# Unpaced slot scatters, a later last batch and single row loads in an attention and mixture-of-experts kernel

## The chip, the cores and the metric

The kernel runs on one core of one Trainium2 chip. The metric is the device time of one execution in microseconds. Three runs of the kernel before gave 550.91, 548.15 and 549.37 us, a median of 549.37.

## What is computed

The input x has 8 batches of 1024 tokens with 128 features, in float32. Two layers follow each other, each with a residual sum:

```
x = x + layernorm(linear_attention(layernorm(x)))          # 16 heads of 8
u = layernorm(x)
logits = (layernorm(u)*ln_scale + ln_bias) @ gate_w.T      # 8 experts
w      = the two largest softmax values, renormalised; 0 for the other experts
y = swiglu(u; shared weights) + sum_e w[:, e] * swiglu(u; Wg[e], Wu[e], Wd[e])   # 128 -> 256 -> 128
x = x + layernorm(y)
```

Each token goes to only two of the eight experts, so 16,384 token rows are computed instead of 65,536.

## The kernel before, in words

**Attention and routing.** Batches go through steps 0 to 7. In a step TensorE (PE) computes attention for one batch, and for the batch before it the shared expert and the router's logits. VectorE (DVE) finds each token's two experts, and a product with a triangular matrix (`ranks`) gives each token its place among the rows of its expert. GpSimd (POOL) then runs `scatter(k)` (line 555) for batch k: 16 indirect DMAs of 128 rows of 144 floats each, which put every token row into `slots_dram`, once for each of its two experts, at the rows named in `slot_i`. They rotate over four semaphores (`lane_out`, LANES = 4). `slots_ready` tells POOL that a batch's slots are known.

**Expert units.** The rows are worked off in 72 units of 256 rows. Units 0 to 31 (N1 = 32) take rows of batches 0 to 4 (FIRST = 5), units 32 to 71 the rest. For a unit n, PE transposes x three units ahead (line 795), multiplies by the gate and up weights (line 806), and multiplies unit n-2 by the down weights (line 816). ScalarE (ACT) copies the transposed x (line 981), takes the silu (line 898), and scales the output into one of four buffers `yb` of four units (line 995). DVE multiplies silu and up (line 1151, `hidden`). POOL writes the output with two indirect DMAs of 128 rows each (`scatter_y`, line 580) to `routed_dram`, where the two results of a token lie side by side.

**Order around the change.** Each engine works its instructions in order, and the order is written out by hand. POOL's is: slot scatters of batches 0 to 5, outputs of units 0 to 3, slot scatters of batch 6 (SEVENTH), outputs of units 4 to 15, slot scatters of batch 7, outputs of units 16 to 71. Within units 0 to 31 the routing of the last two batches is woven in: RANKS_OF names the units ahead of which PE computes `ranks` for batches 6 and 7; T_AT, LOGITS_AT and COUNT_AT those of batch 7's two transposes (line 702), its logits (line 709) and the final count of rows per expert (line 767). On DVE the pieces start at MAIN_FROM, ROUTER_FROM, WEIGHTS_FROM, SLOTS_FROM and TABLE_FROM and advance by up to six steps a unit. On ACT, U_AFTER, UT_AFTER and EXP_AFTER place the corresponding work. Between units 31 and 32 stand the shared expert's products of batches 6 and 7 (`late_stages`, lines 670 and 691).

**The load queue.** SyncE (SP) issues all plain DMAs. After the up product of unit n it loads the weights of unit n+4 (256 KB, `load_weights`, line 421, four places) and the rows of unit n+8 (`load_unit`, line 426). At n = PADS_AFTER it waits for `pads_ready` and issues eight writes of pad rows (`load_pads`, line 433). Rows for units 32 to 39 are loaded after the pads and all slot scatters have landed. At n = 55 it waits until the outputs of 48 units have landed and then issues the row loads of the final stage (`load_pair`, line 439, 1024 KB each, four places). The load of batch 4 is to wait for `pair_read` 1, since it reuses the place of batch 0. Loads of batches 5 to 7 follow once every output scatter has landed.

**The final stage.** From unit 58 on (C_FROM) DVE advances it by up to three steps after each unit (C_STRAND): `c_sums` adds the two results of a token (line 1583), adds the shared expert's output (line 1587) and takes statistics (line 1591). `c_norm` scales (line 1005 on ACT, 1619 on DVE), `c_add` adds the residual (line 1627), and SP stores.

Of the kernel before, what the change touches and what calls it, by code (L numbers as in the profile page):

```python
# [20 lines left out]
B, S = 8, 1024  # L21
NT = S // P
# [14 lines left out]
SLOTS_C = 4  # L37
LANES = 4
# [9 lines left out]
FIRST = 5  # L48
# [19 lines left out]
STRAND = 6  # L68
SPLIT_STEP = 47
SEVENTH = B - 2  # L70
RANKS_OF = {5: SEVENTH, 19: B - 1}
T_AT = (13, 14)
LOGITS_AT = 15
COUNT_AT = 21
X_AHEAD = 3
SLOTS7_FROM = 5
MAIN_FROM = 5
ROUTER_FROM = 15
WEIGHTS_FROM = 18
SLOTS_FROM = 19  # L80
TABLE_FROM = 21
U_AFTER = 12
UT_AFTER = (13, 14)
EXP_AFTER = {4: SEVENTH, 17: B - 1}
SCATTER_AFTER = (4, 16)
PADS_AFTER = 25
TABLE1_AT = tuple(range(1, 36, 2))
C_LOAD_AT = (55, 60)
C_FROM = 58
C_STRAND = 3  # L90
C_NORM_AFTER = (66, 67)
# [8 lines left out]
def program(nc, x, w_qkv, b_qkv, w_proj, b_proj, ln_scale, ln_bias, gate_w, wg, wu, wd, swg, swu, swd, out):  # L100
# [13 lines left out]
    with ctx:  # L114
# [6 lines left out]
        def sem(name):  # L121
            return ctx.enter_context(nc.semaphore(name))
# [185 lines left out]
        lane_out = [sem("lane_out0"), sem("lane_out1"), sem("lane_out2"), sem("lane_out3")]  # L308
# [20 lines left out]
        def pair(b):  # L329

            places = [wgu[1][:, i * NE // 2:(i + 1) * NE // 2, :].rearrange("p e n -> p (e n)") for i in range(2)]
            places += [pad_rows[:, :, :].rearrange("p e n -> p (e n)")[:, 0:2 * NT * E], u_rows_[:, :, :, :].rearrange("p a t n -> p (a t n)")[:, 0:2 * NT * E]]
            return places[b % SLOTS_C].rearrange("p (t c n) -> p t c n", c=2, n=E)
# [42 lines left out]
        def _(sp):  # L376
# [42 lines left out]
            def load_weights(n):  # L419
                e = sp.value_load(unit_ei[0:1, n:n + 1], min_val=0, max_val=NE - 1)  # L420
                sp.dma_start(w_unit(n), wgu_dram[ds(e, 1), :, :].rearrange("e p n -> p (e n)")).then_inc(w_in[n % WSLOTS], 16)

            def load_unit(n):
                i = n % QU
                row = sp.value_load(unit_row[0:1, n:n + 1], min_val=0, max_val=SLOTS - W)
                sp.dma_start(xb[i // HALF][:, TILES * (i % HALF):TILES * (i % HALF) + TILES, :],
                             slots_dram[ds(row, W), :].rearrange("(p t) n -> p t n", t=TILES)).then_inc(xb_in[i], 16)

            def load_pads():
                sp.wait_ge(pads_ready, 1)  # L430
                for e in range(NE):
                    row = sp.value_load(pad_i[0:1, e:e + 1], min_val=0, max_val=NE * CAP - W)
                    sp.dma_start(slots_dram[ds(row, W), :].rearrange("(p t) n -> p (t n)", t=TILES),
                                 pad_rows[:, TILES * e:TILES * e + TILES, :].rearrange("p t n -> p (t n)")).then_inc(pads_in, 16)

            def load_pair(b):
                if b >= SLOTS_C:
                    sp.wait_ge(pair_read, b - SLOTS_C + 1)
                sp.dma_start(pair(b).rearrange("p t c n -> p (t c n)"), routed_v[b, :, :]).then_inc(pair_in[b % SLOTS_C], 16)
# [18 lines left out]
            for n in range(UNITS - WSLOTS):  # L458
                sp.wait_ge(up_ps, n + 1)
                if n + WSLOTS == N1:  # L460
                    sp.wait_ge(table_ready, 2)
                load_weights(n + WSLOTS)
                if n == PADS_AFTER:
                    load_pads()
                if n % HALF == 0:
                    sp.wait_ge(yi_sb, n // HALF + 1)
                if n + QU < N1 or N1 <= n < UNITS - QU:
                    load_unit(n + QU)
                if n == N1 - 1:
                    sp.wait_ge(pads_in, 16 * NE)  # L470
                    for lane in lane_out:
                        sp.wait_ge(lane, 16 * (2 * NT // LANES) * B)
                    for i in range(QU):
                        load_unit(N1 + i)
                if n == C_LOAD_AT[0]:

                    for place in y_out:
                        for done in place:
                            sp.wait_ge(done, 16 * HALF * (FIRST_DONE // HALF // YB))
                    for b in range(SLOTS_C):  # L480
                        load_pair(b)
                if n == C_LOAD_AT[1]:
                    load_pair(SLOTS_C)

            for place in range(YB):
                for done in y_out[place]:
# [9 lines left out]
        def _(pool):  # L496
            g = nc.gpsimd
            n = [0]
# [56 lines left out]
            def scatter(k, par):  # L555
                pool.wait_ge(slots_ready, k + 1)
                for i in range(2 * NT):
                    t, c = divmod(i, 2)
                    at = k * 2 * NT + i
                    if k < SEVENTH and i % LANES == 0 and at:  # L560
                        for lane in lane_out:
                            pool.wait_ge(lane, 16 * (at // LANES))
                    if k == SEVENTH and i == 0:
                        for lane in lane_out:
                            pool.wait_ge(lane, 16 * (at // LANES))
                    elif k >= SEVENTH and i % 2 == 0:

                        for one in (at - 3, at - 2):
                            pool.wait_ge(lane_out[one % LANES], 16 * (one // LANES + 1))
                    g.indirect_dma_start(slots_dram, bass.IndirectOffsetOnAxis(ap=slot_i[par][:, c * NT + t:c * NT + t + 1], axis=0),  # L570
                                         u_row[par][:, t, :], None).then_inc(lane_out[i % LANES], 16)

# [22 lines left out]
        def _(pe):  # L595
# [159 lines left out]
            def last_batch(n):  # L755

                m = B - 1
                if n in T_AT:
                    transpose_u(m, m % 2, [T_AT.index(n)])
                if n == LOGITS_AT:  # L760
                    pe.wait_ge(uT_sb, 2 * B)
                    logits(m)
                if n in RANKS_OF:
                    ranks(RANKS_OF[n])
                if n == COUNT_AT:
                    pe.wait_ge(oh_ready, B + 1)
# [111 lines left out]
        def _(act):  # L878
# [81 lines left out]
            def last_batch(n):  # L960

                m = B - 1
                if n == U_AFTER:
                    u_of(m, m % 2)
                if n in UT_AFTER:
                    uT_of(m, UT_AFTER.index(n))
                if n in EXP_AFTER:
                    router_exp(EXP_AFTER[n])

# [71 lines left out]
        def _(dv):  # L1041
# [460 lines left out]
            def second_last(m):  # L1502

                yield from slots(m, m % 2)
                yield from weights(m, m % 2)
# [128 lines left out]
            def last_stage():  # L1634
# [24 lines left out]
                for g in range(C_HELD + 1, len(C_GROUPS)):  # L1659
# [7 lines left out]
                    if g == last_g:  # L1667
# [6 lines left out]
            tail = weights(m, m % 2)  # L1674
            pieces = [(0, seventh, min(RANKS_OF)), (SLOTS7_FROM, second_last(SEVENTH), T_AT[0]), (MAIN_FROM, main(B, B % 2), T_AT[0]),
                      (ROUTER_FROM, router(m, m % 2), max(RANKS_OF)), (WEIGHTS_FROM, some(tail, 5), N1),
                      (SLOTS_FROM, closing(m, tail), COUNT_AT), (TABLE_FROM, table2(), PADS_AFTER)]
            dv.wait_ge(sy_ps, 2 * (B - LATE))
# [46 lines left out]
```

## Time and profile before

| | |
|---|---|
| Time of the profiled execution | 550.29 us |
| Its span, first to last instruction | 548.6 us |
| Median of three runs | 549.37 us |
| PE busy | 428.6 us (78% of the span) |
| DVE busy | 344.0 us (63%) |
| POOL busy | 277.1 us (51%) |
| ACT busy | 273.3 us (50%) |
| Mean granted clock of PE | 0.939 |

The shares are averages over very different stretches: PE has no work from about 501 us on, and POOL has little but slot scatters until 268 us. A timeline row gives the start, the duration, and in brackets the idle time ahead of it and what ended that. POOL's durations are those of preparing an indirect DMA; the transfer lands later.

### The profile page before, as it was taken

The numbers are of one execution on the slowest core, as the hardware profiler recorded it, in microseconds if no ns is written. First come the engines' busy times: TensorE is split into PE (matmuls) and PEld (weight loads), VectorE is DVE, ScalarE is ACT, GpSimd is POOL, SyncE is SP. The second block draws the span as 40 slices with busy tenths as digits, with TensorE's granted clock in tenths as the row PEclk, the third lists the DMA queues.
The fourth block names the chain that finished last, engine by engine and source line by source line (L and its number), as shares of the span: only waits on it lengthen the run. The fifth ranks groups of instructions, "written<-read, shape, count | busy, mean of one in ns | idle before, by whom it ended". The sixth has DMA issues, their size and how long they took to land.

```text
span 548.6 us, 9418 instructions
## 1 busy us (share of the span) xinstructions
PE 428.6 (78%) x2503; PEld 343.0 (63%) x2511; DVE 344.0 (63%) x1495; ACT 273.3 (50%) x627; POOL 277.1 (51%) x330
## 2 busy tenths in 40 slices
PE   0875979888798979788997999799999995995000
PEld 0453646566556646467996999656999994995000
DVE  6587888889798887984572484122323224886197
ACT  2452465654637474644754655333555552476504
POOL 6000003555453555535655677567777777778300
PEclk9987999999999999997999999999999998999555
DMA  8970000111010111135765565514767679841472
GB/s 254 313 253 0 1 2 23 44 45 43 33 45 34 43 45 38 39 109 164 201 183 150 158 191 195 163 60 133 220 183 204 197 212 410 261 138 45 167 278 115
DMA packets 41623, 73.93 MB, mean 135 GB/s; under 512 B 8803, under 2 KB 23782, under 8 KB 40422
## 3 DMA queue, kind: packets, MB, share of 16 engines
q1 hardware_dynamic: 32870, 54.48, 33.0%
q0 software_dynamic: 8704, 18.89, 9.5%
q8 instruction: 19, 0.31, 0.3%
q14 instruction: 30, 0.25, 0.1%
HBM read 45.82 MB, written 27.53 MB: 134 GB/s over the span
## 4 chain that ended last, share of the span: by engine, by line
PE 51%; DVE 17%; DMA 8%; ACT 8%; issue 6%; POOL 5%; SPq 4%; DVEq 1%; POOLq 0%
PE bank_g L806 9%; PE bank_p L806 8%; PE bank_h L816 8%; POOL routed_dram L580 5%; PE bank_p L653 4%; PE bank_g L670 3%; PE bank_h L691 3%; PE bank_p L614 3%; DVE hid_s L1162 3%; PE bank_t L795 2%; PE bank_h L670 2%; PE bank_t L709 2%; DMA wgu_slots<-wgu_dram 2%; PE bank_t L658 2%; DMA keep<-in_L_attn_x 2%
## 5 line engine op out<-in xcount | busy, mean ns | idle before, releaser
L570 POOL DMA_INDIRECT slots_dram<-u_rows,slot_i x128 | 123.4, 964 | 191.1 <-issue 105.8
L806 PE MATMUL bank_g<-xbT,wgu_slots 128*128 128x256 f32 x288 | 76.2, 388 | 8.0 <-DMA wgu_slots<-wgu_dram 6.2
L816 PEld LDWEIGHTS bank_h<-wdn,hid_s 128*128 128x128 f32 x576 | 75.3, 192 | 4.4 <-issue 0.8
L816 PE MATMUL bank_h<-wdn,hid_s 128*128 x576 | 75.8, 275 | 0.4 <-issue 0.4
L806 PE MATMUL bank_p<-xbT,wgu_slots 128*128 128x256 f32 x288 | 75.6, 386 | 0.0
L806 PEld LDWEIGHTS bank_p<-xbT,wgu_slots 128*128 128x128 f32 x288 | 55.9, 194 | 7.9
L1151 DVE TENSOR_TENSOR hid_s<-act_s,bank_p 128x512 f32<-128x512 f32 x36 | 24.7, 687 | 54.7 <-PE bank_p L806 49.1
L1151 DVE TENSOR_TENSOR hid_s<-q_e,bank_p 128x512 f32<-128x512 f32 x36 | 24.7, 685 | 53.5 <-PE bank_p L806 49.2
L806 PEld LDWEIGHTS bank_g<-xbT,wgu_slots 128*128 128x128 f32 x288 | 50.3, 195 | 12.4 <-DMA wgu_slots<-wgu_dram 6.4
L580 POOL DMA_INDIRECT routed_dram<-pk,yi x40 | 40.8, 1020 | 12.2 <-issue 10.7
L580 POOL DMA_INDIRECT routed_dram<-pqT,yi x40 | 39.8, 996 | 12.2 <-issue 11.6
L653 PE MATMUL bank_p<-wqkv,xnT 128*128 128x256 f32 x128 | 38.2, 399 | 0.0
L580 POOL DMA_INDIRECT routed_dram<-wgu_slots,yi x32 | 31.9, 997 | 9.8 <-issue 6.7
L580 POOL DMA_INDIRECT routed_dram<-att,yi x32 | 31.7, 992 | 9.8 <-issue 7.9
L1078 DVE BATCH_NORM_STATS2 st_r<-keep 128x6 f32<-128x128 f32 x128 | 30.4, 282 | 4.2 <-DMA keep<-in_L_attn_x 3.4
L1005 ACT ACTIVATE keep<-keep,shift,r_c 128x128 f32<-128x128 f32 x56 | 21.9, 483 | 22.1 <-DVE shift L1608 22.1
L981 ACT ACTIVATE xbT<-bank_t 128x256 f32<-128x256 f32 x72 | 27.4, 384 | 10.7 <-PE bank_t L795 10.7
L911 ACT ACTIVATE xn<-keep,nb_r,r_r 128x128 f32<-128x128 f32 x64 | 25.4, 481 | 10.9 <-DVE nb_r L1225 10.9
L652 PE MATMUL bank_p<-bias_bf,ones_bf 128*128 128x256 bf16 x64 | 18.3, 287 | 15.1 <-DVE pqT L1132 13.7
L670 PE MATMUL bank_g<-uT,swgu 128*128 128x512 f32 x56 | 29.3, 604 | 0.8 <-issue 0.8
L898 ACT ACTIVATE act_s<-bank_g 128x512 f32<-128x512 f32 x36 | 21.5, 597 | 14.8 <-PE bank_g L806 14.8
L670 PE MATMUL bank_h<-uT,swgu 128*128 128x512 f32 x56 | 27.9, 601 | 0.0
(258 smaller groups left out, 879.6 us busy)
## 6 DMA issues: line engine op xcount, KB each, us to landing
wgu_slots<-wgu_dram SPq DMA_DIRECT2D x72, 256.0 KB, 2.9
xn<-slots_dram SPq DMA_DIRECT2D x36, 144.0 KB, 2.8
v<-slots_dram SPq DMA_DIRECT2D x36, 144.0 KB
keep<-in_L_attn_x SPq DMA_DIRECT2D x8, 512.0 KB, 4.3
pair_rows<-routed_dram SPq DMA_DIRECT2D x4, 1024.0 KB, 6.1
out_dram<-keep SPq DMA_DIRECT2D x8, 512.0 KB, 7.6
wgu_dram<-keep SPq DMA_DIRECT2D x2, 1024.0 KB, 5.3
slots_dram<-u_rows,slot_i POOLq DMA_INDIRECT x128, 2.3
```

The source lines that it names most:

```text
L570: g.indirect_dma_start(slots_dram, bass.IndirectOffsetOnAxis(ap=slot_i[par][:, c * NT + t:c * NT + t + 1], axis=0), u_row[par][:, t, :], N ...
L580: g.indirect_dma_start(routed_dram, bass.IndirectOffsetOnAxis(ap=yi[:, h % (2 * YB), at:at + 1], axis=0), yb[h % YB][:, at, :], None).then ...
L653: last = mm(o, xnT[:, t * P:(t + 1) * P], wqkv[:, E:3 * E], start=False, stop=True)
L670: last = mm(bank[:, :], swgu[:, which * INTER + c * P:which * INTER + (c + 1) * P], uT_at(m)[:, half * 512:(half + 1) * 512], start=True, ...
L806: last = mm(bank[i % 2][:, c * W:(c + 1) * W], w_unit(i)[:, which * INTER + c * P:which * INTER + (c + 1) * P], xbT[:, i % XDEEP, :], star ...
L816: last = mm(bank[:, t * E:(t + 1) * E], hid[:, i % XDEEP, c * W + t * P:c * W + (t + 1) * P], wdn[:, ds(e, 1), c * E:(c + 1) * E].rearrang ...
L898: A(act_g[n % XDEEP], bank_g[n % 2][:, :], ACT.Silu).then_inc(silu, 1)
L911: ins = A(xn[:, t, 0:E], kept(f, t * E, (t + 1) * E), ACT.Identity, bias=nb_r[par][:, NT + t:NT + t + 1], scale=r_r[par][:, 2 * NT + t:2 * ...
L981: A(xbT[:, n % XDEEP, :], x_bank(n)[:, 0:W], ACT.Copy).then_inc(xbT_sb, 1)
L1005: ins = A(y, y, ACT.Identity, bias=shift[:, g % 2, at], scale=r_c[:, g % 2, at])
L1078: k = inc(v.bn_stats(st(t), src(t)))
L1151: v.tensor_tensor(hid[:, n % XDEEP, :], act_g[n % XDEEP], bank_p[n % 2][:, :], ALU.mult).then_inc(hid_sb, 1)
```

## The change

The waits inside the slot scatters of batches 5, 6 and 7 are left out: only the wait ahead of the first one of a batch is kept. In the kernel before, batch 5 waited ahead of every fourth, and batches 6 and 7 ahead of every second. The pieces of the last batch's routing are placed in later units: the transposes at units 14 and 16, logits at 18, ranks at 21, the count at 24, pads after 27, with their counterparts on DVE and ACT. Row loads of batches 0 to 4 in the final stage are issued one each at n = 55, 57, 59, 61 and 63, where four stood at 55 and one at 60.

```diff
-RANKS_OF = {5: SEVENTH, 19: B - 1}
-T_AT = (13, 14)
-LOGITS_AT = 15
-COUNT_AT = 21
+RANKS_OF = {5: SEVENTH, 21: B - 1}
+T_AT = (14, 16)
+LOGITS_AT = 18
+COUNT_AT = 24
-ROUTER_FROM = 15
-WEIGHTS_FROM = 18
-SLOTS_FROM = 19
-TABLE_FROM = 21
+ROUTER_FROM = 18
+WEIGHTS_FROM = 21
+SLOTS_FROM = 22
+TABLE_FROM = 24
-UT_AFTER = (13, 14)
-EXP_AFTER = {4: SEVENTH, 17: B - 1}
+UT_AFTER = (14, 16)
+EXP_AFTER = {4: SEVENTH, 20: B - 1}
-PADS_AFTER = 25
+PADS_AFTER = 27
-C_LOAD_AT = (55, 60)
+C_LOAD_AT = (55, 57, 59, 61, 63)
...
-                    for b in range(SLOTS_C):
-                        load_pair(b)
-                if n == C_LOAD_AT[1]:
-                    load_pair(SLOTS_C)
+                if n in C_LOAD_AT:
+                    load_pair(C_LOAD_AT.index(n))
...
-                    if k < SEVENTH and i % LANES == 0 and at:
+                    if i % (LANES if k < FIRST else 2 * NT) == 0 and at:
                         for lane in lane_out:
                             pool.wait_ge(lane, 16 * (at // LANES))
-                    if k == SEVENTH and i == 0:
-                        for lane in lane_out:
-                            pool.wait_ge(lane, 16 * (at // LANES))
-                    elif k >= SEVENTH and i % 2 == 0:
-
-                        for one in (at - 3, at - 2):
-                            pool.wait_ge(lane_out[one % LANES], 16 * (one // LANES + 1))
```

## Rows read from the trace of the kernel before

**Rows 1.** Page: rate of data in 40 slices; chain that ended last, by engine.
```profile
GB/s 254 313 253 0 1 2 23 44 45 43 33 45 34 43 45 38 39 109 164 201 183 150 158 191 195 163 60 133 220 183 204 197 212 410 261 138 45 167 278 115
...
PE 51%; DVE 17%; DMA 8%; ACT 8%; issue 6%; POOL 5%; SPq 4%; DVEq 1%; POOLq 0%
```

**Rows 2.** PE timeline, gate products of units 11, 12, 18 and batch 7's pieces.
```profile
283.73 1.03 PE L806 MATMUL bank_g<-xbT,wgu_slots 128*128 128x256 f32 x4
...
286.57 1.03 PE L806 MATMUL bank_g<-xbT,wgu_slots 128*128 128x256 f32 x4
...
290.59 0.65 PE L702 MATMUL bank_t<-ident,u_rows 128*128 128x128 f32 x4 [1.23 <-DVE u_rows L1237]
...
300.05 1.95 PE L709 MATMUL bank_t<-gate_c,xnT 128*128 128x8 f32 x16 [1.20 <-ACT xnT L920]
...
310.62 1.03 PE L806 MATMUL bank_g<-xbT,wgu_slots 128*128 128x256 f32 x4
```

**Rows 3.** DVE timeline: slots of batch 6 ready, experts of batch 7, slots ready.
```profile
274.14 0.17 DVE L1331 SCALAR_TENSOR_TENSOR u_rows<-r_exp,wden 128x8 f32<-128x8 f32 x1
...
310.90 0.23 DVE L1303 TENSOR_TENSOR oh_bf<-oh 128x64 bf16<-128x64 f32 x1
...
318.53 0.17 DVE L1331 SCALAR_TENSOR_TENSOR u_rows<-r_exp,wden 128x8 f32<-128x8 f32 x1
```

**Rows 4.** PE timeline: gate product of unit 30.
```profile
346.62 1.10 PE L806 MATMUL bank_g<-xbT,wgu_slots 128*128 128x256 f32 x4 [1.88 <-issue]
```

**Rows 5.** SP timeline: the eight pad writes, weights of units 57 and 60.
```profile
334.62 8.47 SPq L433 DMA_DIRECT2D slots_dram<-pad_rows  x8
...
440.60 0.33 SPq L421 DMA_DIRECT2D wgu_slots<-wgu_dram  x1
...
452.39 0.35 SPq L421 DMA_DIRECT2D wgu_slots<-wgu_dram  x1
```

**Rows 6.** PE timeline: gate products of units 60 and 61.
```profile
464.15 2.08 PE L806 MATMUL bank_g<-xbT,wgu_slots 128*128 128x256 f32 x4 [6.16 <-DMA wgu_slots<-wgu_dram]
...
468.81 1.03 PE L806 MATMUL bank_g<-xbT,wgu_slots 128*128 128x256 f32 x4
```

**Rows 7.** Page, DMA issues: KB each, median us to landing.
```profile
wgu_slots<-wgu_dram SPq DMA_DIRECT2D x72, 256.0 KB, 2.9
...
pair_rows<-routed_dram SPq DMA_DIRECT2D x4, 1024.0 KB, 6.1
```

**Rows 8.** POOL groups by line, 238 to 268.5 us: slot scatters of batch 5.
```profile
L570 POOL DMA_INDIRECT slots_dram<-u_rows,slot_i x16 | 15.3, 957 | 19.1 <-DMA slots_dram<-u_rows,slot_i 10.4 <-DVE u_rows L1331 5.1 <-issue 3.7
```

**Rows 9.** POOL timeline: first scatters of each stretch, a slow one, the last.
```profile
279.13 0.95 POOL L570 DMA_INDIRECT slots_dram<-u_rows,slot_i  x1 [0.30 <-issue]
...
308.80 0.96 POOL L580 DMA_INDIRECT routed_dram<-pqT,yi  x1 [0.30 <-issue]
...
339.71 0.96 POOL L570 DMA_INDIRECT slots_dram<-u_rows,slot_i  x1 [0.30 <-issue]
...
366.60 0.95 POOL L580 DMA_INDIRECT routed_dram<-pk,yi  x1 [0.30 <-issue]
...
407.01 0.96 POOL L580 DMA_INDIRECT routed_dram<-pk,yi  x1 [0.30 <-issue]
...
494.33 2.02 POOL L580 DMA_INDIRECT routed_dram<-pk,yi  x1 [0.30 <-issue]
...
512.11 0.95 POOL L580 DMA_INDIRECT routed_dram<-pqT,yi  x1 [0.30 <-issue]
```

**Rows 10.** ACT timeline: output of unit 68, normalisation after unit 71.
```profile
496.74 0.63 ACT L995 ACTIVATE pqT<-bank_h,yw 128x128 f32<-128x128 f32 x2 [1.16 <-PE bank_h L816]
...
502.13 12.40 ACT L1005 ACTIVATE keep<-keep,shift,r_c 128x128 f32<-128x128 f32 x32
```

**Rows 11.** DVE timeline: a residual sum, first sum after the last loads.
```profile
494.31 1.21 DVE L1627 TENSOR_TENSOR keep<-keep 128x1024 f32<-128x1024 f32 x1
...
519.76 1.23 DVE L1583 TENSOR_TENSOR pair_rows<-pair_rows 128x1024 f32<-128x1024 f32 x1 [10.05 <-DMA pair_rows<-routed_dram]
```

## The prediction, written before the changed kernel ran

> **What bounds the kernel now.** I read the page's shares and the chain of waits first, then the timelines of PE, POOL and SP around the three edits, then the end. The chain's shares say mostly PE [rows 1], but the reader is to see that two engines take turns. PE sets the pace up to its last down product near 501 us. The end is POOL's: the output scatter of unit 71 starts only at 512.11 [rows 9], though ACT wrote its output before 502.13, where its next work begins [rows 10]. POOL is some 10 us behind. Loads of batches 5 to 7 wait for that last scatter, DVE waits for them until 519.76 [rows 11], and a fixed tail of 548.6 - 519.76 = 28.8 us follows. So what counts is when POOL's last scatter ends, and that is the later of two things: POOL's own backlog, and PE's production of the last outputs. The change touches both.
>
> POOL's backlog comes from the slot scatters. Back to back, POOL needs (407.01 - 366.60) / 32 = 1.263 us a scatter [rows 9], 2.53 us for a unit's two. PE needs 286.57 - 283.73 = 2.84 us a unit [rows 2], so POOL gains only 0.31 us a unit and never makes up what it lost.
>
> **The scatters without pauses.** Sixteen at 1.263 are 20.2 us. Batch 5 has 10.4 us of waits for its own earlier scatters [rows 8]; the usual gap of 0.3 stays at three places, so 9.5 go. It then would reach unit 0's output before ACT has written it: here PE and ACT are the cover, and outputs 0 to 3 are set by them. Batch 6 next needs its slots, ready at 274.14 + 0.17 = 274.3 [rows 3]. So batch 6 starts at 274.5 instead of 279.13 and ends at 294.7 instead of 308.80 [rows 9]. Outputs 4 to 15 keep their 339.71 - 308.80 = 30.9 us, which gives 325.6. Are batch 7's slots ready by then? They were ready at 318.7, in unit 19, which starts one unit of 2.84 after 310.62 plus about 0.3 for the ranks, 313.7; that is 5.0 after its start [rows 2, 3]. Moved to unit 22 (three units later, 8.5 us) and with the 3.0 us that PE wins below, they are ready at 324.2, 1.4 us before POOL asks. Batch 7 runs from 325.6 to 345.8 instead of 366.60: POOL is 20.8 us ahead. Outputs 16 to 31 end at 386.2 instead of 407.01.
>
> How a run of 16 slot scatters without a wait behaves, no row shows: batch 5 has only four in a row. From below, they could run at the 1.263 of the output scatters, 64 KB each against 72. From above, nothing is gained and a batch takes the 29.7 (batch 6) or 26.9 us (batch 7) of now [rows 9]. I take 1.263: the output scatters go 32 in a row at it beside the same weight loads. Moving 72 KB per 1.26 us is 58 GB/s more, where the slices of this stretch show 130 to 220 and one slice reaches 410 [rows 1].
>
> A rule speaks against this. The Trainium skill (DMA: Bandwidth & Descriptors, "Issuing engines are not separate DMA queues") says that DMAs from all issuers end up on the same 16 DMA engines and interleave. By it alone denser scatters could delay the weight loads. That case is the last rival; the sum above stands without it.
>
> **The last batch's routing, two units apart.** Units 12 to 18 take 310.62 - 286.57 = 24.05 us. Six units are 17.04, and the pieces themselves 0.65 twice and 1.95, 3.25 together; 3.8 is left, of which three waits (1.23 for DVE's rows, one alike, 1.20 for ACT's copy) are nearly all [rows 2]. With the transposes at 14 and 16 and logits at 18, PE comes 2.84 us after DVE's and one or two units after ACT's part, so all 3.8 go. Late next are the ranks: before, they stood two units after the router's last unit, now one (router in 18 to 20, ranks at 21). In unit 17 (start 307.8, one unit before 310.62) DVE finished the expert masks at 311.1, 3.3 us after the start [rows 2, 3]; PE would ask after 2.6 (a unit without the two transposes), so it waits 0.7. Both bounds: 0 if DVE is a bit quicker, 2.0 if its pieces lag by a further product. I take 0.8 with the restart. Behind PE's wait only its own transposes queue. Net 3.0.
>
> The pads: on SP the eight writes take 8.47 us [rows 5] and stood ahead of the weights of unit 30; PE then idles 1.88 [rows 4]. Now they come after the weights of unit 31, the last that PE needs before the late shared products, which give more than 20 us of cover for units 32 to 35. The stall goes, 1.9. SP's waits for all slot scatters, formerly until batch 7 landed, now end near 348 and no longer come last; the eight unit loads behind them keep their place ahead of unit 32. DVE's table finishes in unit 26, before n = 28 needs it. The idle goes to 0 in the good case and stays 1.9 in the bad one. PE is then 4.9 us earlier at unit 32.
>
> **The row loads.** Before, four loads of 1 MB stood in SP's queue ahead of the weights of unit 60, issued at 452.39 [rows 5] and landed 11.7 later, where 2.9 is usual [rows 7]. PE idled 6.16, then ran unit 60 at the lower clock: 468.81 - 464.15 = 4.66 instead of 2.84, 1.8 more [rows 6]. Together 8.0. With one load ahead of the next weights the landing must stay below 8.8 us: unit 60 was due at 464.15 - 6.16 = 458.0, so unit 53 started seven units of 2.84 before, at 438.1; its turn's weights were issued at 440.60 [rows 5], 2.5 after, and are needed four units, 11.36, after the start. Four cost 11.7 - 2.9 = 8.8, so one costs 2.2, and 5.1 us is covered. In two units SP and POOL move 1.05 + 0.52 + 0.29 + 0.26 = 2.1 MB in 5.68 us, 375 GB/s, close to the 410 seen [rows 1], so this is the least sure term: between 8.0 and 0, and at the bad end four stalls. I take 8.0. DVE uses batch b three units after the unit whose turn issues it. The issue comes some 4 us after that unit's start (its weights at 2.5, then a unit load, about 1.5 for both: an estimate), DVE's use at 8.5 + 2.5; that leaves 7 us for a landing of 6.1 [rows 7]. Where a load lands at 8, DVE waits about a microsecond, and PE has a unit's slack before it needs the next `hidden`. So zero, up to 2 if the slack is used up. The 48-unit wait ahead of the loads no longer stops SP, since POOL has caught up by then.
>
> **The sum.** PE is 4.9 + 8.0 = 12.9 us earlier at the end. POOL reaches output 32 at 386.2. Output 68 was ready near 497.1 [rows 10]; 36 units of 2.84 and the 8.0 before it, output 32 was at 386.9, and 4.9 less is 382.0. It is 4 us behind, and closes that in 4 / 0.31 = 13 units. From then on POOL follows PE. Output 68 is ready at 496.74 + 0.37 - 12.9 = 484.2 [rows 10]; from it eight scatters come faster than PE's pace allows POOL to rest, 8 x 1.263 = 10.1, so the last ends at 494.0. Some scatters beside DVE's wide sums take longer: the one at 494.33 took 2.02 us instead of 0.96, and the sum at 494.31 ran exactly beside it [rows 9, 11]. For these I add 1.8, bounds 0 and 4. The last scatter ends at 495.8 instead of 513.06, 17.3 us earlier. ACT's 12.4 us of normalising after unit 71 end at 502.13 - 12.9 + 12.4 = 501.6, before DVE's first late sum at 502.5, so the tail moves along whole.
>
> A page disagrees with the 1.8. The Trainium skill (SBUF — State Buffer, "Who interferes with whom") holds that a `tensor_tensor` with both inputs in SBUF takes the read interface only, and infers that making descriptors does not need it, so such a sum would not stall an indirect DMA. By that rule the sum is 1.8 us lower. This trace's 2.02 speaks against it, and I go by the row.
>
> Profiled execution: 550.29 - 17.3 = 533.0. That execution is 0.92 above the median of the runs, so 532.1 is my number for the median.
>
> **The rivals.**
> 1. The forecast, 532.1: chance 0.66. Its own range is 529.5 (no slow scatters, no ranks wait) to 537 (4 us of slow scatters, 2.7 lost in ranks or a short stall).
> 2. One weight load still comes late. Rate near 375 GB/s speaks for it, the 5.1 below 8.8 against it. PE then wins only 4.9 at the end, and perhaps pays a stall of the clock: output 68 at 492.2, last scatter 503.8, 9.3 earlier, 540. Chance 0.17.
> 3. The unwaited scatters run no faster, because POOL itself is held when too many are under way. POOL stays 20 us behind: its last scatter remains at 513 minus 0 to 4, and 546 to 549 follows. The 32 output scatters in a row speak against. Chance 0.06. That a wait remains elsewhere (the change doing nothing) belongs here.
> 4. A better split: batch 7's slots earlier and all waits smaller, 528.5. Chance 0.06.
> 5. Slower. DVE stands in order, and each row load arrives after DVE's turn. If each lands 11 us after issue, as the weights behind four did, DVE waits 4.2, PE loses about that plus 1.8 for the clock, five times: 30 us, less the 17.3, 562. It decides against the change once DVE's waits pass 17 us in sum, 3.5 a load. By the interleaving rule above denser traffic makes this likelier. Chance 0.05.
>
> **How the numbers follow.** The range takes in the forecast, case 4 and most of case 2: 528.5 to 541, leaving out about 0.16. A measurement of this kernel can tell about 0.5%, 2.7 us, from no change. Faster: 0.66 + 0.17 + 0.06 and a third of case 3 give 0.91; same 0.04; slower 0.05.
>
> **What would show it.** Right: L570's 16 scatters of batches 5 to 7 at 1.26 spacing with no DMA releaser; L702 and L709 without idle; unit 30 without idle; no idle on PE at unit 60 and PEclk at full there; POOL waiting for ACT outputs from about unit 45 on; last scatter at 496. Wrong: idle before a gate product released by `wgu_slots`, DVE idle before line 1583 during units 60 to 68, or POOL still without waits to the end.

## The result, and the profile after

Three runs of the changed kernel took 533.62, 534.76 and 533.83 us, a median of 533.83 where 532.1 was predicted. Against the kernel before (549.37) that is a ratio of 0.9714 [0.9692, 0.9736]: faster, and inside the range. The profiled execution took 533.62 us with a span of 531.9, against 550.29 and 548.6, so 16.7 us are to be found. Line numbers are 9 lower than before from the scatters on, because the waits are gone: L561 is the slot scatter, L571 the output scatter, L797 the gate product.

From the page: the rate of data in 40 slices and the chain by engine. Against [rows 1] POOL's share of the chain fell from 5% to 2% and that of DMA from 8% to 5%, and PE's rose from 51% to 60%.

```profile
GB/s 249 301 294 1 1 2 12 46 39 46 39 40 46 29 45 35 46 34 174 183 188 204 192 180 174 179 212 89 130 206 191 202 194 250 389 295 50 193 261 119
...
PE 60%; DVE 18%; ACT 6%; DMA 5%; issue 3%; SPq 3%; POOL 2%; DVEq 0%; POOLq 0%
```

POOL's timeline: the last of batch 5's slot scatters and unit 0's output, the start of batch 6, of outputs 4 to 15, of batch 7, of outputs 16 to 31, of output 32; then a wait for ACT, two long scatters behind such waits, a third long one, and the last. Columns are start, duration, and in brackets the idle time ahead with what ended it.

```profile
259.03 0.96 POOL L561 DMA_INDIRECT slots_dram<-u_rows,slot_i  x1 [0.30 <-issue]
263.35 0.96 POOL L571 DMA_INDIRECT routed_dram<-pk,yi  x1 [3.37 <-ACT pk L986]
...
276.08 0.96 POOL L561 DMA_INDIRECT slots_dram<-u_rows,slot_i  x1 [1.04 <-DVE u_rows L1322]
...
296.29 0.96 POOL L571 DMA_INDIRECT routed_dram<-pqT,yi  x1 [0.30 <-issue]
...
326.63 0.95 POOL L561 DMA_INDIRECT slots_dram<-u_rows,slot_i  x1 [0.30 <-issue]
...
347.43 0.96 POOL L571 DMA_INDIRECT routed_dram<-pk,yi  x1 [0.30 <-issue]
...
387.85 0.95 POOL L571 DMA_INDIRECT routed_dram<-pk,yi  x1 [0.31 <-issue]
...
437.24 0.96 POOL L571 DMA_INDIRECT routed_dram<-pk,yi  x1 [0.62 <-ACT pk L986]
...
463.27 1.74 POOL L571 DMA_INDIRECT routed_dram<-att,yi  x1 [1.10 <-ACT att L986]
...
482.44 1.65 POOL L571 DMA_INDIRECT routed_dram<-pk,yi  x1 [0.40 <-ACT pk L986]
...
493.24 1.91 POOL L571 DMA_INDIRECT routed_dram<-pqT,yi  x1 [0.30 <-issue]
495.45 0.96 POOL L571 DMA_INDIRECT routed_dram<-pqT,yi  x1 [0.30 <-issue]
```

The reader is to see, against [rows 9]: batch 6 from first scatter to the next output takes 20.21 us instead of 29.67, batch 7 takes 20.80 instead of 26.89. From 437 us on idle time of more than 0.31 us ahead of a scatter is ended by ACT: POOL follows PE. The last scatter ends at 496.41 instead of 513.06, and these 16.65 us are the whole gain.

PE's timeline: gate product of unit 12, batch 7's two transposes, its logits, the gate product of unit 18, the ranks, and the gate products of units 30, 32 and 60.

```profile
288.05 1.03 PE L797 MATMUL bank_g<-xbT,wgu_slots 128*128 128x256 f32 x4
...
293.51 0.60 PE L693 MATMUL bank_t<-ident,u_rows 128*128 128x128 f32 x4
...
299.62 0.60 PE L693 MATMUL bank_t<-ident,u_rows 128*128 128x128 f32 x4
...
305.73 1.85 PE L700 MATMUL bank_t<-gate_c,xnT 128*128 128x8 f32 x16
...
307.69 1.03 PE L797 MATMUL bank_g<-xbT,wgu_slots 128*128 128x256 f32 x4
...
316.84 0.20 PE L710 MATMUL bank_t<-oh_bf,tri 128*128 128x64 bf16 x1 [0.69 <-DVE oh_bf L1294]
...
342.51 1.03 PE L797 MATMUL bank_g<-xbT,wgu_slots 128*128 128x256 f32 x4
...
375.96 1.03 PE L797 MATMUL bank_g<-xbT,wgu_slots 128*128 128x256 f32 x4
...
453.65 1.03 PE L797 MATMUL bank_g<-xbT,wgu_slots 128*128 128x256 f32 x4
```

No piece of the routing but the ranks has idle time ahead of it [rows 2], unit 30 has none [rows 4], and the 6.16 us ahead of unit 60 [rows 6] are gone. DVE's timeline: the instruction that makes batch 7's slots ready, the only wait for a row load, and the first sum after the last loads. ACT's: output of unit 68, and the normalising after unit 71.

```profile
324.05 0.17 DVE L1322 SCALAR_TENSOR_TENSOR u_rows<-r_exp,wden 128x8 f32<-128x8 f32 x1
...
450.96 1.23 DVE L1574 TENSOR_TENSOR pair_rows<-pair_rows 128x1024 f32<-128x1024 f32 x1 [0.30 <-DMA pair_rows<-routed_dram]
...
503.09 1.23 DVE L1574 TENSOR_TENSOR pair_rows<-pair_rows 128x1024 f32<-128x1024 f32 x1 [5.70 <-DMA pair_rows<-routed_dram]
```

```profile
484.42 0.62 ACT L986 ACTIVATE pqT<-bank_h,yw 128x128 f32<-128x128 f32 x2 [1.16 <-PE bank_h L807]
...
489.81 12.41 ACT L996 ACTIVATE keep<-keep,shift,r_c 128x128 f32<-128x128 f32 x32
```

### The profile page after: what moved, and what is told of

It reads as the page before. It is cut to its first block, busy times and chain, and to the rows that moved or that the text cites. A ratio compares the mean times of both kernels' runs of the same rounds, so it can differ in the third digit from the quotient of the medians.

```text
span 531.9 us, 9399 instructions
## 1 busy us (share of the span) xinstructions
PE 425.9 (80%) x2503; PEld 342.3 (64%) x2511; DVE 343.9 (65%) x1495; ACT 272.7 (51%) x627; POOL 273.8 (51%) x330
## 4 chain that ended last, share of the span: by engine, by line
PE 60%; DVE 18%; ACT 6%; DMA 5%; issue 3%; SPq 3%; POOL 2%; DVEq 0%; POOLq 0%
PE bank_g L797 11%; PE bank_p L797 11%; PE bank_h L807 11%; PE bank_p L644 4%; PE bank_g L661 3%; PE bank_h L682 3%; PE bank_t L786 3%; PE bank_p L605 3%; DVE hid_s L1153 3%; PE bank_h L661 2%; PE bank_t L700 2%; PE bank_t L649 2%; DMA keep<-in_L_attn_x 2%; POOL routed_dram L571 2%; ACT L907 1%
## 5 line engine op out<-in xcount | busy, mean ns | idle before, releaser
L561 POOL DMA_INDIRECT slots_dram<-u_rows,slot_i x128 | 123.7, 966 | 167.7 <-issue 111.2
L797 PE MATMUL bank_g<-xbT,wgu_slots 128*128 128x256 f32 x288 | 75.0, 383 | 0.0
L797 PE MATMUL bank_p<-xbT,wgu_slots 128*128 128x256 f32 x288 | 74.8, 382 | 0.0
L797 PEld LDWEIGHTS bank_p<-xbT,wgu_slots 128*128 128x128 f32 x288 | 55.3, 192 | 7.7
L797 PEld LDWEIGHTS bank_g<-xbT,wgu_slots 128*128 128x128 f32 x288 | 49.7, 193 | 3.8
L571 POOL DMA_INDIRECT routed_dram<-pk,yi x40 | 39.0, 975 | 18.0 <-ACT pk L986 9.8
L571 POOL DMA_INDIRECT routed_dram<-pqT,yi x40 | 39.3, 981 | 13.5 <-issue 9.8
L571 POOL DMA_INDIRECT routed_dram<-att,yi x32 | 31.6, 987 | 11.6 <-issue 9.6
L571 POOL DMA_INDIRECT routed_dram<-wgu_slots,yi x32 | 30.9, 965 | 10.8 <-issue 7.3
L972 ACT ACTIVATE xbT<-bank_t 128x256 f32<-128x256 f32 x72 | 27.3, 383 | 9.1 <-PE bank_t L786 9.1
L643 PE MATMUL bank_p<-bias_bf,ones_bf 128*128 128x256 bf16 x64 | 18.3, 285 | 15.3 <-DVE pqT L1123 13.8
L884 ACT ACTIVATE v<-bank_p 128x256 f32<-128x256 f32 x32 | 12.3, 383 | 31.4 <-PE bank_p L644 31.4
```

The costliest lines, as they stand in the source:

```text
L571: g.indirect_dma_start(routed_dram, bass.IndirectOffsetOnAxis(ap=yi[:, h % (2 * YB), at:at + 1], axis=0), yb[h % YB][:, at, :], None).then ...
L643: mm(o, ones_bf[:, 0:P], bias_bf[:, E:3 * E], start=True, stop=False)
L797: last = mm(bank[i % 2][:, c * W:(c + 1) * W], w_unit(i)[:, which * INTER + c * P:which * INTER + (c + 1) * P], xbT[:, i % XDEEP, :], star ...
L972: A(xbT[:, n % XDEEP, :], x_bank(n)[:, 0:W], ACT.Copy).then_inc(xbT_sb, 1)
```

## The experiments

They fall into two groups. Four kernels ran on a chip where the kernel before takes 548.7 us, as in the case. The other eight ran on four chips where the same kernel before takes 630 to 633 us. Absolute times of the two groups can't be compared, and ratios only with care. In the diffs, three dots stand for lines that are not shown.

### Where the kernel before takes 549 us

**without_loads**: the changed kernel with the four row loads at 55 and one at 60 again.

```diff
-C_LOAD_AT = (55, 57, 59, 61, 63)
+C_LOAD_AT = (55, 60)
...
```

> Changed kernel with four row loads at unit 55 and one at 60 again. Theory: PE idles about 6 us at unit 60 and runs it at half clock, 8 us in all, and now the end follows PE: 541.5. Rival 1 (POOL's slack hides it): 534 to 536. Rival 2: the stall is shorter because SP no longer waits for the outputs of 48 units before the loads: 539 to 540.

Measured 542.07 us, ratio 0.9882 [0.9848, 0.9915] to the kernel before; 8.2 above the changed kernel. PE's timeline of this kernel, gate products of units 60 and 61:

```profile
458.85 2.08 PE L799 MATMUL bank_g<-xbT,wgu_slots 128*128 128x256 f32 x4 [6.57 <-DMA wgu_slots<-wgu_dram]
...
464.47 1.03 PE L799 MATMUL bank_g<-xbT,wgu_slots 128*128 128x256 f32 x4
```

The stall is back where it was, 6.57 us, and the unit behind it takes 5.62 instead of 2.84, 2.8 more, at a granted clock of 0.51. From unit 12's gate product to unit 71's PE takes 205.67 us where the changed kernel takes 196.17, 9.5 more; it reached unit 12 1.5 us earlier (286.52), so the last scatter starts at 503.43, 8.0 later. With the backlog gone, a stall of PE there goes straight to the end.

**without_routing**: batch 7's routing and the pads at the units of before, the rest as changed.

```diff
-RANKS_OF = {5: SEVENTH, 21: B - 1}
-T_AT = (14, 16)
-LOGITS_AT = 18
+RANKS_OF = {5: SEVENTH, 19: B - 1}
+T_AT = (13, 14)
+LOGITS_AT = 15
...
-PADS_AFTER = 27
+PADS_AFTER = 25
...
```

> Changed kernel with the last batch's routing and pads where they were. Theory: PE loses the 3.0 us of waits at units 13 to 15 (less the new wait of 0.7) and the 1.9 before unit 30, and the end follows PE: 538.7. Rival (the units' slack hides it): 534 to 535.

Measured 539.69 us, ratio 0.9829 [0.9794, 0.9864]; 5.9 above the changed kernel. PE's timeline, the transposes and logits:

```profile
291.10 0.66 PE L693 MATMUL bank_t<-ident,u_rows 128*128 128x128 f32 x4 [1.46 <-DVE u_rows L1228]
...
295.89 0.63 PE L693 MATMUL bank_t<-ident,u_rows 128*128 128x128 f32 x4 [1.30 <-ACT xnT L911]
...
300.56 1.95 PE L700 MATMUL bank_t<-gate_c,xnT 128*128 128x8 f32 x16 [1.21 <-ACT xnT L911]
```

All three waits are back, unit 30 waits 2.44 us, and from unit 12 to unit 71 PE takes 204.28 us, 8.1 more than the changed kernel; it too began earlier (286.85), and its last scatter starts at 502.36, 6.9 later. So what PE loses 190 to 250 us before the end reaches the end once POOL has no backlog: the last scatter is late by the 8.1 less the 1.2 of the earlier start.

**batch5_paused**: batch 5 waits ahead of every fourth scatter again.

```diff
-                    if i % (LANES if k < FIRST else 2 * NT) == 0 and at:
+                    if i % (LANES if k <= FIRST else 2 * NT) == 0 and at:
```

> Changed kernel with the pauses of batch 5 alone put back (ahead of every fourth). Theory: batch 6 starts 4.6 us later, POOL is 8 to 9 us behind at output 32 and closes 0.31 us a unit, so it has caught up near unit 60: within 1 us of 533.8. Rival (every us of POOL counts): 538.

Measured 533.72 us, ratio 0.9724 [0.9686, 0.9763], no different from the changed kernel. POOL's timeline: it is late at unit 0 and at batch 6 (279.36 where the changed kernel has 276.08), and the last scatter starts at 495.54 against 495.45.

```profile
264.05 0.95 POOL L561 DMA_INDIRECT slots_dram<-u_rows,slot_i  x1 [3.30 <-DMA slots_dram<-u_rows,slot_i]
...
269.11 0.96 POOL L571 DMA_INDIRECT routed_dram<-pk,yi  x1 [0.30 <-issue]
...
279.36 0.96 POOL L561 DMA_INDIRECT slots_dram<-u_rows,slot_i  x1 [0.30 <-issue]
```

At output 32 POOL is 2.9 us later than in the changed kernel (390.77 against 387.85), and unit by unit it makes that up: at unit 56 it first has idle time that ACT ends. Of the scatter edit, batch 5's part is worth nothing here.

**two_loads**: two row loads ahead of one set of weights, at 55 and 59, the fifth at 63.

```diff
-C_LOAD_AT = (55, 57, 59, 61, 63)
+C_LOAD_AT = (55, 59, 63)
...
-                    load_pair(C_LOAD_AT.index(n))
+                    first = 2 * C_LOAD_AT.index(n)
+                    for b in range(first, min(first + 2, FIRST)):
+                        load_pair(b)
```

> Changed kernel with row loads of batches 0 and 1 at unit 55, 2 and 3 at 59, 4 at 63. My sum priced a load of 1 MB ahead of the weights at 2.2 us, which would land the weights 2.9 + 4.4 = 7.3 us after issue, below the 8.8 they may take: no idle on PE, 533.8. Rival (each load ahead costs its own 1 MB at the full rate of about 400 GB/s seen with all four, 2.6 us, plus the rest of the traffic, 3.4): 9.7 us, PE idles 1 us twice and may lose the clock, 535.5 to 538.

Measured 534.02 us, ratio 0.9745 [0.97, 0.9791]: the same as single loads. SP's and PE's timelines, the weights behind two row loads and the product that needs them:

```profile
443.10 0.81 SPq L439 DMA_DIRECT2D pair_rows<-routed_dram  x2
445.03 0.35 SPq L421 DMA_DIRECT2D wgu_slots<-wgu_dram  x1
```

```profile
453.36 1.13 PE L799 MATMUL bank_g<-xbT,wgu_slots 128*128 128x256 f32 x4 [0.28 <-DMA wgu_slots<-wgu_dram]
```

The weights came 8.3 us after their issue, and unit 60 waited 0.28 (unit 64, behind the second pair, waited 0.63 with no releaser named). So two loads use up the cover almost exactly. They cost the weights behind them 8.3 - 2.9 = 5.4 us. What one costs stands in the changed kernel's own trace, DMA issues between 445.2 and 445.4 us:

```profile
wgu_slots<-wgu_dram SPq DMA_DIRECT2D x1, 256.0 KB, 6.6
```

That is 3.7 us for one (the weights behind the third and the fifth row load take 6.7), 5.4 for two, 8.8 for four in the kernel before, and 10.5 for four in without_loads, where the weights issued at 445.42 arrived at 458.85. The price is not proportional to the number: the first load costs more than the 2.2 that the prediction got by dividing the price of four. Four stall PE, two just don't.

### Where the kernel before takes 630 us

**only_scatters** and **only_scatters_2**: of the change only the waits are left out. The second is the same kernel on another chip, sent because the first came out slower where every theory had it faster.

```diff
-                    if k < SEVENTH and i % LANES == 0 and at:
+                    if i % (LANES if k < FIRST else 2 * NT) == 0 and at:
...
```

> Kernel before with one edit: no pauses inside the slot scatters of batches 5 to 7. Theory (the end is the later of POOL's backlog and PE's production of outputs): POOL's 20 us of backlog go, PE's outputs come as late as before, so the last output scatter ends at 497.1 + 8 x 1.263 + about 1 = 508.3 instead of 513.1, and the time falls by about 5 us to 544.5. PE still idles about 6 us at unit 60. Rival 1 (the backlog was the whole bound): all of the gain, 533 to 535. Rival 2 (three edits with a share each): 17 us split by what they save on PE and POOL, some 544, but then the two other edits alone must show a gain too.

> Kernel before with one edit, no pauses inside the slot scatters of batches 5 to 7, once more, since the first run of it was on a chip on which ACT, DVE and SP stood still for many microseconds at a time and the kernel before took 630 us. On a chip where the kernel before takes 549. Theory (the end is the later of POOL's backlog and PE's outputs): about 5 us faster, 543.5 to 545.5, with PE still idle some 6 us at unit 60. Rival 1 (the backlog was the whole bound): 533 to 535. Rival 2 (back to back scatters hold up the instruction streams of the other engines, as on the other chip): 555 or more. If the kernel before takes 630 here, both kernels repeat the numbers of the first run.

Measured 644.23 against 630.27 us, ratio 1.0226 [1.018, 1.0273], and 651.15 against 631.1, ratio 1.0304 [1.024, 1.0368]. The page of the first and ACT's and DVE's timelines:

```profile
PE 43%; DVE 17%; another core or an unknown queue 14%; ACT 8%; issue 6%; DMA 5%; SPq 5%; DVEq 0%; POOL 0%; POOLq 0%; ACTq 0%
```

```profile
263.41 0.60 ACT L913 ACTIVATE uT<-bank_t 128x512 f32<-128x512 f32 x1 [17.74 <-remote]
...
324.00 0.62 ACT L988 ACTIVATE pqT<-bank_h,yw 128x128 f32<-128x128 f32 x2 [16.28 <-remote]
```

```profile
311.41 0.69 DVE L1144 TENSOR_TENSOR hid_s<-act_s,bank_p 128x512 f32<-128x512 f32 x1 [13.38 <-remote]
```

On these chips ACT and DVE stand still for 6 to 32 us at a time between 245 and 440 us, with nothing of this program that the profile could name as the releaser ("remote"). The views of the 549 us chips have not one such wait. Of PE's busy time, 122.4 us fall between 245 and 440 us, where the changed kernel has 188.2. The expectations had this kernel faster by about 5 us or more on a 549 us chip; on these chips it is slower. My theory of the kernel says nothing of such standstills, and it failed here. On a 549 us chip this kernel was not measured.

**only_routing** and **only_loads**, the other two parts alone.

```diff
-RANKS_OF = {5: SEVENTH, 19: B - 1}
+RANKS_OF = {5: SEVENTH, 21: B - 1}
...
-C_LOAD_AT = (55, 60)
+C_LOAD_AT = (55, 57, 59, 61, 63)
...
```

> Kernel before with one edit: the last batch's routing and the pads later. Theory: PE is 5 us earlier at unit 32, but POOL's scatters run as before without a gap up to the end, so no change: 549, within 1.5. SP's wait for the outputs of 48 units grows from 1.4 to some 6 us and gives PE's gain back at unit 60. Rival (shares that add up): about 5 us faster, 544.

> Kernel before with one edit: one row load at a time. Theory: PE's idle at unit 60 and its slow unit go (8 us on PE), and the end does not move, since POOL ends as before: 549, within 1.5. Rival (shares that add up): 8 us faster, 541.

Measured 631.22 us, ratio 1.0027 [1.0001, 1.0054], and 622.15, ratio 0.9874 [0.983, 0.9917]. The routing alone brought nothing. The loads are worth 8.1 us, where the expectation was no change. Both expectations took it that POOL is behind, and here it is not. POOL's timeline of only_loads at output 32:

```profile
455.89 0.96 POOL L578 DMA_INDIRECT routed_dram<-pk,yi  x1 [31.50 <-ACT pk L993]
```

In only_routing the same wait is 26.38 us. So neither run tests the backlog theory; that PE's stall at unit 60 counts where POOL is not behind agrees with without_loads. ACT's, POOL's and PE's timelines of only_loads show where the standstills lie:

```profile
414.01 0.63 ACT L993 ACTIVATE att<-bank_h,yw 128x128 f32<-128x128 f32 x2 [23.21 <-remote]
```

```profile
379.26 0.95 POOL L578 DMA_INDIRECT routed_dram<-pk,yi  x1 [0.30 <-issue]
...
410.86 0.96 POOL L578 DMA_INDIRECT routed_dram<-att,yi  x1 [0.31 <-issue]
414.65 0.96 POOL L578 DMA_INDIRECT routed_dram<-att,yi  x1 [2.83 <-ACT att L993]
```

```profile
389.13 1.15 PE L814 MATMUL bank_h<-wdn,hid_s 128*128 x8 [1.10 <-ACT att L993]
415.07 2.07 PE L814 MATMUL bank_h<-wdn,hid_s 128*128 x8 [24.79 <-ACT att L993]
```

ACT stood from 390.8 to 414.0 while POOL issued one scatter after another, 0.30 us apart, from 379 to 411.8, and it went on 2.2 us after POOL had paused. The product that ACT's row reads was PE's, and it had ended at 390.28; PE in its turn then waited 24.79 us for ACT. So ACT stood with its input made. In the stretches of this kernel in which POOL still waits between slot scatters, no standstill of 5 us or more lies.

**without_scatters** and **without_scatters_2**: routing and loads changed, the waits kept.

```diff
-                    if i % (LANES if k < FIRST else 2 * NT) == 0 and at:
+                    if k < SEVENTH and i % LANES == 0 and at:
...
```

> Changed kernel with the pauses inside the slot scatters put back. Theory: POOL's backlog is back and ends at 511 to 513, so nothing is left of the gain: 547 to 549. PE waits at unit 60 again, since SP stands before the outputs of 48 units. Rival (shares that add up): 538 to 540.

> Changed kernel with the pauses inside the slot scatters put back, once more for the same reason. Theory: POOL's scatters run without a gap from the pauses to the end and finish at 511 to 513, so nothing is left of the gain: 547 to 549, and SP stands before the outputs of 48 units for 5 us or more, so that PE idles again at unit 60. Rival (shares that add up): 538 to 540.

Measured 619.62 us, ratio 0.9791 [0.9735, 0.9847], and 624.85, ratio 0.9884 [0.9801, 0.9967]. The expectation was that nothing of the gain is left; it too took POOL to be behind, and POOL's wait for ACT at output 32 is 27.3 and 27.4 us here. With the waits kept, the other two parts bring 1.2 to 2.1% on these chips. The next run has the waits left out as well.

**both_later**: the changed kernel with two moves that were to bring 2 us more: DVE's residual sums come after the last output scatter, and the ranks one unit later.

```diff
-                    adds = c_add(g - 1, n[0]) if g else iter(())
+                    adds = iter(())
...
-RANKS_OF = {5: SEVENTH, 21: B - 1}
+RANKS_OF = {5: SEVENTH, 22: B - 1}
...
```

> Changed kernel with two further edits. First, the residual sums of batches 0 to 2 on DVE wait until all output scatters have landed, since in the changed kernel's trace the scatters at 482.44 and 493.24 us, begun inside such a sum, took 1.65 and 1.91 us instead of 0.96 and POOL had no slack there: 1.6 us, and the three sums (3.7 us) fit ahead of 503 where DVE waits for rows anyway. Second, batch 7's ranks at unit 22 instead of 21 (slots from 23, count at 25, table from 25, pads after 28), which takes away PE's wait of 0.69 us and its restart: 0.8 us. Theory: 533.8 - 2.4 = 531.4. Rival 1 (a slow scatter is slow whatever DVE does): 533 for the first edit. Rival 2 (batch 7's slots come 2.8 us later and POOL does not make that up): 533 to 534. If the chip is one on which the kernel before takes 630: by the single edits measured there (scatters 1.023 to 1.030, loads 0.987, routing 1.003) the product is 1.013 to 1.020, 638 to 643, slower than before; rival there (with the loads spread, the unpaused scatters do no harm): 0.97, 611.

Measured 635.31 against 632.47 us, ratio 1.0056 [1.0027, 1.0085]. It landed on a 630 us chip, so the 2 us could not be seen; whether it beats the changed kernel on a 549 us chip is open. It is the nearest thing to the whole change on such a chip, and by it the whole change is worth nothing there; the changed kernel itself was not run on one.

**paced**: without_scatters with a pause of POOL ahead of every second unit from 4 to 47, to break the unbroken runs of output scatters.

```diff
...
+                if 4 <= n < 48 and n % 2 == 0:
+                    hp, kp = divmod(n - 1, HALF)
+                    for done in y_out[hp % YB]:
+                        pool.wait_ge(done, 16 * (HALF * (hp // YB) + kp + 1))
```

> Changed kernel with the pauses inside the slot scatters of batches 5 to 7 put back, and further ones added: ahead of every second unit from 4 to 47, POOL waits until the output scatters of the unit before have landed, so that before unit 48 it never issues more than four scatters without a pause. It tests why the chips on which the kernel before takes 630 us are slow. Theory for these: during long runs of scatters without a pause ACT, DVE and SP get no new instructions there, and stand still for 6 to 32 us with everything ready (seven traces show it, always inside such a run). With pauses the standstills of over 5 us go, and only POOL's own pauses cost: about 1 us a unit, the time falls from 630 to 565 to 590. Rival (the standstills sit at places of the program and have nothing to do with POOL): they stay, and the pauses come on top, 635 or more. If the chip is one on which the kernel before takes 549: POOL is slower by 1 us a unit over 44 units on top of its old backlog, 575 to 590, slower than before.

Measured 604.44 against 632.89 us, ratio 0.9552 [0.9495, 0.961]: the fastest kernel of this group. DVE's and ACT's longest standstills between 245 and 440 us:

```profile
316.33 0.69 DVE L1153 TENSOR_TENSOR hid_s<-act_s,bank_p 128x512 f32<-128x512 f32 x1 [6.88 <-remote]
```

```profile
356.05 0.63 ACT L997 ACTIVATE wgu_slots<-bank_h,yw 128x128 f32<-128x128 f32 x2 [5.32 <-remote]
```

Between 245 and 440 us PE is busy for 175.8 us, against 134.2 and 128.5 in the two runs of without_scatters, whose longest standstills there are 31.7 and 27.5 us. From unit 48 on, where this kernel has no added pauses, POOL issues scatters without a pause from 488.5 to 525.7 us, and there a long standstill is back, in DVE's timeline:

```profile
527.52 0.69 DVE L1153 TENSOR_TENSOR hid_s<-q_e,bank_p 128x512 f32<-128x512 f32 x1 [13.66 <-remote]
```

So in the traces the long standstills go with unbroken scatters, and more pauses help, though paced ran on a chip of its own. The sum of such waits over all engines and the whole span fell much less: it is 123 us, against 139 and 127 in the two runs of without_scatters, and 147 and 178 in those of only_scatters. Pauses shorten the single standstill and don't remove the cause, and the gain was overrated (565 to 590 was expected). Why ACT and DVE stand no run told.

## Why the prediction was right

**Scatters back to back.** The step held: batch 6 lasted 20.21 us and batch 7 20.80 where 20.2 was forecast. Its starts were 276.08, 326.63, 347.43 and 387.85 where 274.5, 325.6, 345.8 and 386.2 were forecast. Most of the difference is from before batch 6: PE was 1.5 us later at unit 12 (288.05 against 286.57 [rows 2]), and with it ACT's output 0 and DVE's slots of batch 6. The six traces of this group reach unit 12 between 286.52 and 288.05, batch5_paused latest together with the changed kernel, and are as far apart at 238 us already; why was not settled. Rival 3 falls.

That the edit is needed for the gain was not measured on a 549 us chip. What bears it out there is indirect. In the trace of the kernel before, POOL never has more than 0.32 us of idle time ahead of a scatter from 366.60 us to the end. From output 32 at 407.01 [rows 9] its 80 scatters at 1.263 can't end before 407.01 + 79 x 1.263 + 0.95 = 507.7. So by this estimate the edits on PE and on the row loads could bring at most 513.06 - 507.7 = 5.3 us without the one on POOL. The other evidence is POOL's timeline after the change, in which the backlog is gone from 437 us on, and without_loads and without_routing, whose losses reach the end.

**The routing.** Right in mechanism, a little short in size. The three waits are gone, the ranks wait 0.69 where 0.8 with the restart was taken, slots are ready at 324.05 + 0.17 = 324.2, as forecast. Units 12 to 18 take 19.64 us instead of 24.05, 4.4 less where 3.8 was counted. The mis-sized term is that of the pieces, 3.25 together: their durations overlap those of the next instructions, and what they add to six units is 19.64 - 17.04 = 2.6. From unit 12 to unit 32 PE takes 87.91 us instead of 93.56: 5.65 won, 4.9 forecast.

**The row loads.** Right. From unit 60 to 71, with the stall, PE takes 30.57 us instead of 38.55: 7.98 won, 8.0 forecast. Two terms behind it were mis-sized: one load ahead costs the weights 3.7 us instead of 2.2 (two_loads), and they had 453.65 - 445.29 = 8.4 us until their use instead of 8.8. That left 8.4 - 6.6 = 1.8 us of cover where 8.8 - 5.1 = 3.7 was counted; it was still enough. The two row loads whose landing the trace tells (443.84 and 466.26) took 7.1 and 7.3 us instead of 6.1, and DVE waited 0.30 once: rivals 2 and 5 fall.

**When POOL catches up.** Forecast after 13 units, at 45; found at units 50 and 51, and the first longer wait for ACT is at 437.24, unit 51. This size was off. ACT finished the first half of output 32 at 383.04 and POOL took the output up at 387.85, 4.8 later where 386.2 - 382.0 = 4.2 was forecast (taken as 4); a later start by 0.3 is usual even when POOL is not behind. The rate was right: by unit 43 only 1.35 of the 4.8 us was left, 0.31 less with each unit. Then POOL lost 1.1 us at unit 44. POOL's timeline:

```profile
419.22 0.95 POOL L571 DMA_INDIRECT routed_dram<-att,yi  x1 [1.39 <-issue]
```

ACT had written that output before 417.4, so this wait has another cause, which the profile does not name; batch5_paused has no such wait there. At 0.31 a unit it takes 3.5 units to make up. POOL still caught up well before the end. batch5_paused began unit 32 with 7.6 us and had 0.5 left at unit 55, so some 6 us more than in the changed kernel would have lasted to the end.

**The end.** The first half of output 68 was ready at 484.42 + 0.37 = 484.8 where 484.2 was forecast. PE won 13.8 us from unit 12 on instead of 12.9, but began 1.5 later. POOL came to it 0.87 us after that, at 485.66, having lost 0.69 to a slow scatter at 482.44; eight scatters at 1.263 less the last gap are 9.8, and the slow one at 493.24 adds 0.95: 485.66 + 9.8 + 0.95 = 496.41. The delays beside the 9.8 are 0.87 + 0.95 = 1.8, as forecast, so the end at 496.41 instead of 495.8 is the 0.6 of output 68. The tail from DVE's first late sum is 531.9 - 503.09 = 28.8 us as before, and ACT's normalising ends at 502.22, ahead of 503.09. In all the last scatter ends 16.65 us earlier instead of 17.3. That the total came so close is in part luck: PE won 0.9 us more than forecast and began 1.5 us later. Rival 4 (528.5) falls with the measured time.

## What to carry to other kernels

Where two engines take turns in setting the end, ask of each which one is behind and by how much it can gain per round: an edit on the other brings little until the backlog is gone (here, by the estimate above, at most 5.3 of the 13.8 us that PE won), and nearly its full length afterwards. In a queue that serves small urgent loads and large ones, price the large ones by the urgent load behind them, against the time until it is used, and measure that price for one load as well as for all together: here one cost 3.7 us, two 5.4 and four 8.8 to 10.5; one or two fit, four don't. And measure on more than one chip before a wait is called superfluous: here the unpaused scatters were part of a change that gained 2.9% on one chip, and alone they lost 2 to 3% on two others.

## What the hardware showed that was not expected

**A scatter begun inside one of DVE's wide sums waits for it.** DVE's timeline of the changed kernel, the two wide sums beside the slow scatters at 463.27 and 482.44:

```profile
462.93 1.22 DVE L1574 TENSOR_TENSOR pad_rows<-pad_rows 128x1024 f32<-128x1024 f32 x1
...
482.06 1.21 DVE L1618 TENSOR_TENSOR keep<-keep 128x1024 f32<-128x1024 f32 x1
```

The scatters end at 465.01 and 484.09, 0.86 and 0.82 us after the sums (464.15 and 483.27), and last 1.74 and 1.65 us instead of 0.96. The 2.02 of before ends 0.83 after its sum [rows 9, 11]. The Trainium skill (SBUF — State Buffer, "Who interferes with whom") infers the opposite, that a `tensor_tensor` with both inputs in SBUF leaves descriptor generation alone. By its rule these scatters would take 0.96; the measurement decides, and the three long ones near the end (463.27, 482.44 and 493.24) cost 2.4 us together. The 14 kept traces have 64 scatters that began 0.03 to 1.0 us after the start of such a 128x1024 sum: every one ended 0.83 to 0.86 us after the sum and took 1.05 to 2.00 us. Of ten that began within 0.02 us of the sum's start, only the 2.02 of before was held; the other nine took 0.96, like the one at 477.15. In both_later, whose residual sums come after the last scatter, none of the last twelve scatters took more than 0.96. So the sums are the cause of these long scatters; what the end would gain without them was not measured on a 549 us chip.

**The same kernel takes 549 us on some chips and 630 on others**, by the traces with standstills of ACT and DVE with unnamed releaser, the long ones mostly during unpaused runs of scatters, and with a mean granted clock of 0.89 to 0.91 instead of 0.94 in the profiled executions. All eight traces taken on these four chips show them; of the kernel before there is no trace from such a chip. Their cause is open.
